# Gathers of a pairwise recommender tower issued in short runs: the first couples in twos, the rest paced by VectorE's product count

## What is computed

```python
e = jnp.stack([tbl_0[ids[:, 0]], tbl_1[ids[:, 1]], ..., tbl_39[ids[:, 39]]], axis=1)   # 512 x 40 x 64
p = e[:, rowidx]                      # the 780 pairs i < j
q = e[:, colidx]
z = jnp.einsum('bie,fie,bif->bi', p, param, q)     # param: 64 x 780 x 64
h = jnp.concatenate([z, dense_ctx], axis=1)
h = jnp.maximum(h @ W_top1 + b_top1, 0.0)
h = jnp.maximum(h @ W_top2 + b_top2, 0.0)
y = h @ W_top3
```

## Time and profile before

| | us |
|---|---|
| median of 3 runs | 548.67 (548.06 to 549.01) |
| the profiled execution | 548.24 |
| its span | 546.4 |
| TensorE matmul busy | 322.2 (59%) |
| VectorE busy | 258.1 (47%) |
| ScalarE busy | 255.2 (47%) |
| GpSimd busy | 185.2 (34%) |

### The profile page before, as it was taken

One profiled execution on the slowest core, in us unless ns is written; L12 is line 12 of the kernel. 1 busy time (PEld: TensorE's weight loads), 2 busy tenths in 40 slices (PEclk: granted clock), 3 DMA queues, 4 the chain that ended last, 5 costly groups with the idle time before them and its releaser, 6 DMA issues.

```text
span 546.4 us, 7416 instructions
## 1 busy us (share of the span) xinstructions
PE 322.2 (59%) x2318; PEld 165.8 (30%) x2318; DVE 258.1 (47%) x262; ACT 255.2 (47%) x1961; POOL 185.2 (34%) x192
## 2 busy tenths in 40 slices
PE   0402000220003200299999999899779999999988
PEld 0201000000001000155455544454454344444645
DVE  0000000000000000389899988855437999998590
ACT  1000000000002100389999969734687999995632
POOL 6777777777777760000000000000001122232030
PEclk9998555565555755599999999999889999999999
DMA  2221111211112110174324220032124242420000
GB/s 59 46 50 30 26 26 26 55 26 26 26 25 62 26 26 1 39 268 124 125 89 148 88 95 10 11 92 76 46 95 173 95 143 79 172 95 1 1 2 0
DMA packets 12937, 35.60 MB, mean 65 GB/s; under 512 B 4705, under 2 KB 5985, under 8 KB 11618
## 3 DMA queue, kind: packets, MB, share of 16 engines
q1 hardware_dynamic: 7778, 29.88, 16.4%
q0 software_dynamic: 5120, 5.25, 5.0%
HBM read 35.12 MB, written 0.00 MB: 64 GB/s over the span
## 4 chain that ended last, share of the span: by engine, by line
PE 34%; another core or an unknown queue 24%; issue 19%; ACT 13%; DVE 8%; POOL 1%; DMA 1%; DVEq 0%
ACT prod L658 11%; PE upsum L537 9%; PE upsum L532 7%; DVE prod L622 6%; PE zbank L489 6%; PE abank L444 5%; PE abank L423 1%; DVE z L596 1%; POOL emb L396 1%; PE upsum L501 1%; ACT xT L637 1%; PE upsum L505 1%; PE abank L469 1%; PE upsum L573 1%
## 5 line engine op out<-in xcount | busy, mean ns | idle before, releaser
L658 ACT ACTIVATE prod<-prod 128x64 f32<-128x64 f32 x944 | 227.0, 250 | 8.1 <-issue 7.2
L658 ACT ACTIVATION_READ_ACCUMULATOR prod<-prod 128x1 f32 x944 | 185.3, 196 | 7.7 <-issue 7.7
L396 POOL DMA_INDIRECT emb<-tbl,rows_id x160 | 151.5, 947 | 50.2 <-issue 48.5
L622 DVE TENSOR_TENSOR prod<-upsum,emb 128x1024 f32<-128x1024 f32 x98 | 116.8, 1220 | 107.1 <-remote 68.5
L537 PE MATMUL upsum<-w,xT 64*128 64x512 f32 x392 | 106.0, 641 | 102.3 <-issue 59.1
L405 POOL TENSOR_TENSOR prod<-prod 128x512 f32<-128x512 f32 x26 | 32.9, 1271 | 290.4 <-DVE prod L622 290.4
L622 DVE TENSOR_TENSOR prod<-upsum,xT 128x1024 f32<-128x1024 f32 x82 | 97.7, 1219 | 67.2 <-remote 40.0
L637 ACT ACTIVATE xT<-abank 128x256 f32<-128x256 f32 x40 | 15.1, 378 | 220.1 <-remote 129.3
L532 PE MATMUL upsum<-xT,w 64*128 64x256 f32 x656 | 88.3, 397 | 4.9 <-DVE prod L622 2.6
L537 PEld LDWEIGHTS upsum<-w,xT 64*128 64x128 f32 x392 | 33.8, 191 | 140.3 <-issue 81.2
L532 PEld LDWEIGHTS upsum<-xT,w 64*128 64x128 f32 x656 | 60.3, 190 | 35.9 <-issue 16.8
(11 more groups left out here) (46 smaller groups left out, 132.0 us busy)
## 6 DMA issues: line engine op xcount, KB each, us to landing
w<-W_top SPq DMA_DIRECT2D x2, 1792.0 KB, 8.2
emb<-tbl,rows_id POOLq DMA_INDIRECT x160
w<-param SPq DMA_DIRECT2D x2, 1248.0 KB
w<-param SPq DMA_DIRECT2D x2, 1152.0 KB
w<-param SPq DMA_DIRECT2D x2, 1120.0 KB
w<-param SPq DMA_DIRECT2D x2, 1024.0 KB
w<-param SPq DMA_DIRECT2D x2, 992.0 KB
w<-param SPq DMA_DIRECT2D x2, 896.0 KB
```

The lines of the kernel that those rows point to most:

```text
L396: pool.indirect_dma_start(emb[:, c, f, :], None, tables[f], bass.IndirectOffsetOnAxis(ap=rows_id[:, c, f:f + 1].bitcast(U32), axis=0),).th ...
L622: dve.tensor_tensor(to.rearrange("p (h q) -> p h q", h=2), t[:], f.broadcast_to([P, 2, BANK]), ALU.mult).then_inc(multiplied, 1)
L658: last = act.activation(ring[:, x * E:(x + 1) * E], ring[:, x * E:(x + 1) * E], ACT.Copy, accum_out=z_view(u)[:, x:x + 1])
```

## The change

The gathers are no longer one row. The first ten couples of half 0 are issued as before, but ahead of couples 2, 4, 6 and 8 GpSimd waits until the four gathers of the couple before have landed (so at most eight are under way). The other 30 couples move into GpSimd's loop over the units, each with a wait until VectorE has finished `u` units (`multiplied`): couples 10 to 19 of half 0, and of half 1, 20 units before their stretch; couples 0 to 9 of half 1 at units 22, 28, 34 and so on to 76, among those of half 0. `H_LAG` goes from 3 to 4. The number of gathers, their size and the order within a couple stay.

```diff
-H_LAG = 3
+H_LAG = 4
+GATHER_FIRST, GATHER_AHEAD, GATHER_OTHER, GATHER_STEP = 10, 20, 22, 6
...
+    gather_at = {}
+    for q in range(NQ):
+        s, n = stretches[q]["s"], stretches[q]["n"]
+        if s == 0 and n >= GATHER_FIRST or s == 1:
+            at = stretches[q]["first"] - GATHER_AHEAD
+            if s == 1 and n < GATHER_FIRST:
+                at = GATHER_OTHER + GATHER_STEP * n
+            assert at <= stretches[q]["first"] - GATHER_AHEAD
+            gather_at.setdefault(max(at, 0), []).append((s, n))
...
-            for s in range(HALVES):
-                for n in range(NC):
-                    for f in (2 * n, 2 * n + 1):
-                        for c in range(s * PER, (s + 1) * PER):
-                            pool.indirect_dma_start(
-                                emb[:, c, f, :], None, tables[f],
-                                bass.IndirectOffsetOnAxis(ap=rows_id[:, c, f:f + 1].bitcast(U32), axis=0),
-                            ).then_inc(gathered[s][n], 16)
+
+            def gather(s, n):
+                for f in (2 * n, 2 * n + 1):
+                    for c in range(s * PER, (s + 1) * PER):
+                        pool.indirect_dma_start(
+                            emb[:, c, f, :], None, tables[f],
+                            bass.IndirectOffsetOnAxis(ap=rows_id[:, c, f:f + 1].bitcast(U32), axis=0),
+                        ).then_inc(gathered[s][n], 16)
+
+            for n in range(GATHER_FIRST):
+                if n >= 2 and n % 2 == 0:
+
+                    pool.wait_ge(gathered[0][n - 1], 16 * 2 * PER)
+                gather(0, n)
             for u in range(NU):
+                for s, n in gather_at.get(u, []):
+
+                    if u:
+                        pool.wait_ge(multiplied, u)
+                    gather(s, n)
                 if units[u]["by"] == "H":
```

## The result

| | before | changed |
|---|---|---|
| median, us | 548.47 (548.06 to 549.01) | 452.51 (449.02 to 453.68) |
| ratio, with its interval | | 0.8239 (0.8194 to 0.8285) |
| profiled execution | 548.24 | 452.29 |
| its span | 546.4 | 450.5 |
| mean granted clock of TensorE | 0.838 | 0.913 |

The change is faster by 17.6%. The forecast was 402 us with a range of 370 to 450: the direction was right, the size was not, and the median lies 2.5 us above the range.

A forecast was written before the change was run, and what follows sets the result against it. It took late TensorE hand-offs, while gathers issued every 1.25 us are worked off at 1.40, to bound the kernel. Span 546.4 - 181 (unit 18 earlier) + 35 (paced-row freezes) = 400.4, plus 1.8 outside: 402 us, range 370 to 450.

The forecast's parts named there:

- the two harmless amounts: Backlog said to delay nothing: up to 1.6 us before unit 18; 10 or 11 gathers per round up to unit 84.
- the freeze: Until 227.68 us in the kernel before, TensorE's reports of ended instructions reach other engines at one per 1.40 us.
- never passes the 1.6 us that did no harm: First ten couples: eight gathers take 11.4 us, are worked off in 11.2, so backlog stays harmless; unit 18 at 63 us.
- rival 4: Whole loop: each group of four gathers freezes it, landing included, 6.5 us for each of 30 groups; 562 us, chance 0.06.
- Units 0 to 17 need some 17 x 1.5 = 26 us of these 60: Before unit 18: the earlier units' work fits within the first ten couples' gather time, so the product stands at 63 us.
- the same harmless eleven: Units 18 to 84: of each 14 to 16 gathers, 10 or 11 harmless, then 7 us frozen; five rounds, 35 us.
- Rival 2: Paced row freezes nearly all through, some 90 of 112 us: 457 us, from 440 to 485; chance 0.10.
- Four fall behind by 0.6 us and have the rest to recover: nothing: Late couples, units 105 to 170: four gathers about every 11 us recover their backlog, cost nothing; 56 us without that cover.
- adds no work: Halvings and H_LAG: the longer lag only moves a reduction by one place on VectorE, costed at 0.
- Rival 1: Whole kernel: short rows never fall far enough behind, so no freeze at all; 371 us, chance 0.14.
- Rival 5: Start of the program: the freeze is unconnected to the gathers and ends at 228 us regardless; 548 us, chance 0.03.
- Rival 3: Paced row: gathers slow to 2.5 us each beside a busy VectorE, 18 couples take 180 us; 461 us, chance 0.06.

The follow-up runs named there:

- e14: The changed kernel as it is, in a set without the freeze: 378.97 us, ratio 1.0297 to the kernel before (367.75).
- e5: The kernel before with H_LAG 4 instead of 3, in a set without the freeze: 370.81 us, ratio 1.0069.
- e12: The kernel before with a 512-column GpSimd memset behind each gather (1.66 us apart, one row), in a set with the freeze: 402.8 us, ratio 0.7349.
- e13: All gathers spaced by 512-column memsets, 35 couples in one row, last five 20 units ahead, H_LAG 4; set without the freeze: 387.25 us, ratio 1.0535.
- e15: The changed kernel with couples 0 to 9 of half 1 at units 40 to 94 instead of 22 to 76, without the freeze: 374.7 us, ratio 1.0231.
- e6: The changed kernel with H_LAG 3 instead of 4, in a set without the freeze: 376.74 us, ratio 1.0263 to the kernel before.
- e7: The kernel before with gathers of 64 rows instead of 128 and a memset of emb ahead, in a set without the freeze: 370.54 us, ratio 1.0088.
- e2: The kernel before with a 384-column GpSimd memset behind each gather (1.55 us apart, one row), in a set with the freeze: 410.72 us, ratio 0.7482.
- e17: All gathers spaced by 512-column memsets, 35 couples in one row, five among the halvings, H_LAG 4; set with the freeze: 387.81 us, ratio 0.7085.
- e4: The changed kernel without its four landing waits, the other 30 couples still paced, in a set with the freeze: 454.69 us, ratio 0.8283.
- e3: The kernel before with landing waits after every eight gathers through all 160, no pacing, in a set with the freeze: 511.17 us, ratio 0.9312.
- e10: The kernel before with gathers of 64 rows instead of 128 and a memset of emb ahead, in a set with the freeze: 555.39 us, ratio 1.0133.

## Why the forecast was right in direction and wrong in size

The steps that failed are the two harmless amounts in the sum, at unit 18 and up to unit 84, and a zero at its end. By the table of stretches, the changed kernel took 50 us more than the forecast: 25 by unit 18, 14 up to unit 84, 0 up to 104, 7 up to 170, 5 to the end. The changed kernel against e14, its own trace without the freeze, has 17.0, 49.2, 0, 6.1 and 0.6 us more, together 73 of the 450.5. The forecast had 35 of these, all between units 18 and 84.

**Unit 18: 88 us instead of 63.** The gathers were issued as forecast: couple 9's last ends at 59.4 (49.67 + 7 x 1.25 + 0.95; forecast 58.8). Two steps behind it failed. First, the step by which the backlog "never passes the 1.6 us that did no harm". The first two pieces do run free, but the product at 42.59 already stands at 39.81 in e14, and the one at 50.50, released by `remote`, at 41.86: 2.8 us are lost around the third piece (26.63 to 36.34), and 6 more by the fourth (38.12 to 47.83). Then come the 16 gathers in a row that I had counted as eight. The harmless start was read from a stretch in which TensorE had next to nothing to report, and carried over to one in which it had. The text named this doubt itself, in rival 4; that TensorE's activity makes the difference is likely, but no run isolates it. Second, "Units 0 to 17 need some 17 x 1.5 = 26 us of these 60" took them for done by the time that couple 9 is there. They were not. TensorE stood from 57 to 73, for a copy that ScalarE made 3.4 us after the last of the 16 gathers:

```profile
72.80 0.38 ACT L662 ACTIVATE xT<-abank 128x256 f32<-128x256 f32 x1 [15.59 <-remote]
73.24 0.69 PE L526 MATMUL upsum<-xT,w 64*64 64x256 f32 x1 [16.08 <-ACT xT L662]
```

Units 11 to 17 were still ahead, and they took the 15.3 us from 72.76 to 88.07.

e14 has its unit 18 at 71.1, so the difference of the two traces is 17 us and not 25. But the 8 us between 63 and 71 have a reason of their own there. A 1.8 MB load of the first layer's weights (L387), with 0.5 MB for the second layer just ahead of it, starts at 52.20, just as couple 8's gathers are under way:

```profile
52.20 0.51 SPq L387 DMA_DIRECT2D w<-W_top  x1
```

```profile
55.00:57.50 2.50, 0.00 (x0) 0.00 (x0) 0.00 (x0) 0.04 (x1) 1.89 (x3) 0.62 1.10 424
57.50:60.00 2.50, 0.00 (x0) 0.00 (x0) 0.00 (x0) 0.00 (x0) 1.89 (x3) 0.50 0.94 392
```

```profile
60.93 0.69 PE L448 MATMUL abank<-ident,emb 128*128 128x128 f32 x2 [7.50 <-DMA emb<-tbl,rows_id]
```

The DMA engines are full at 392 to 424 GB/s, TensorE, VectorE and ScalarE stand, and couple 8, whose last issue ended at 54.14 and would have landed at 55.6, is turned at 60.93: 5 us late. Units 14 to 17 follow it before unit 18 can. The kernel before has the same gap without a freeze (7.07 us in e5), and in e5, e12, e13, e14 and e15 couple 8 is turned 8.7 to 9.2 us after this load starts, though its gathers end anywhere from 47.9 to 62.2. In the changed kernel with the freeze the same load starts only at 74.96, 20 us after couple 8's gathers, and holds back nothing that unit 18 needs:

```profile
74.96 0.50 SPq L387 DMA_DIRECT2D w<-W_top  x1
```

So the load is no part of the 25 us measured; it is what a kernel meets there once the freeze is gone.

**Units 18 to 84: 139 us instead of 125.** The mechanism was the one forecast: gathers almost without a pause, a loop frozen in pieces. But I gave each round of 16 gathers 7 us by the same harmless eleven; 49 us were lost. Rival 2 had this stretch at 90 us of freeze and the kernel at 457. The measured 452.5 came close to its time by another way: 49 of its 90 us of freeze here, the rest elsewhere.

**Units 104 to the end: 12 us more.** "Four fall behind by 0.6 us and have the rest to recover: nothing" was nearly right: 6 us up to unit 170, and 2 more right behind it (units 170 to 180 take 14.8 us instead of 12.9). The rest is `H_LAG`, by which the forecast's step "adds no work" failed: e5 is slower by 0.69% (370.81 to 366.91). All of it lies behind the start of the last unit. There the span has 14.65 us left with lag 3 (before, e6, e7), and with lag 4 between 15.8 and 18.7:

```profile
356.70:372.48 15.78, 12.53 (x70) 8.15 (x70) 1.22 (x2) 3.58 (x9) 0.00 (x0) 1.00 0.00 0
```

```profile
359.07:377.72 18.65, 15.41 (x70) 9.24 (x70) 1.21 (x2) 3.58 (x9) 0.00 (x0) 0.82 0.00 0
```

The first is e15, the second e14, with the same instructions on TensorE and VectorE. The lag itself costs 1.1 us, and 1.6 to 2.9 more where the granted clock is at its lower level for a part of the stretch (mean 0.82 in e14, 0.90 in the changed kernel and e5, 1.00 in e15). Before it TensorE has waited 1.91 us for the last reduction, in e15 as in e14, against 0.18 in e6; what decides between the two clocks is not shown. Lag 3 gives back 1.8 us at the halvings that stand behind gathers (e6 against e14).

**Rivals 1, 3 and 5.** Rival 1 (no freeze, 371) describes the sets without the freeze, where the changed kernel takes 379: 8 us more than rival 1 said, which is the 8 us at unit 18; `H_LAG` and the 4 us that I had allowed for late couples cancel. Rival 5 had the freeze end at 228 us whatever the gathers do; e2 and e12 refute it, since the gathers' distance alone takes the freeze away. Rival 3 fell: gathers beside a busy VectorE keep 0.94 to 0.95 us each (e14, e17).

**What the waits for landings were good for:** beside the pacing, nothing measured (e4). Alone they took 37 us off the kernel before, but no more, since a piece of eight is long enough to freeze the loop (e3). Without the freeze, they and `H_LAG` are the change's cost: unit 18 at 71.1 in e14 against 65.5 in e5 for the waits, and the last stretch for the lag.

**What stays open.** What works gathers off at one per 1.40 us, why reports of other engines wait meanwhile, and what separates the two conditions is not shown. At intervals above 1.40 us the backlog can't grow from gathers alone, yet 1.55 still lost 26 us between units 18 and 84 and 1.66 none. That the reports share the same time with the gathers would fit; no run here tests it. One thing in the trace of the kernel before speaks against engines taking turns at one server, and I had overlooked it: late in the freeze the engines' own instructions go at this pace, and two engines at once.

```profile
183.48 0.27 PE L423 MATMUL abank<-ident,emb 128*128 128x128 f32 x1 [2.21 <-issue]
186.28 0.37 PE L423 MATMUL abank<-ident,emb 128*128 128x128 f32 x1 [2.53 <-issue]
```

```profile
190.46 0.20 ACT L658 ACTIVATION_READ_ACCUMULATOR prod<-prod 128x1 f32 x1 [1.14 <-issue]
191.86 0.26 ACT L658 ACTIVATE prod<-prod 128x64 f32<-128x64 f32 x1 [1.20 <-issue]
193.27 0.20 ACT L658 ACTIVATION_READ_ACCUMULATOR prod<-prod 128x1 f32 x1 [1.15 <-issue]
```

TensorE's two transposes, each with its weight load, are 2.80 us apart, so 1.40 per instruction. Of ScalarE's instructions, 0.2 to 0.3 us long, eleven follow that of 178.56 up to 193.27, across both transposes: eight of them at 1.39 to 1.41 us, the others at 0.7, 0.7 and 2.1. So more is late than the reports, and each engine seems to have a pace of its own of about one instruction per 1.40 us. Why stays open.

A kernel that spaces only the gathers issued beside busy engines, and so would cost less without the freeze, wasn't tried.

## To carry to other kernels

Before moving work around a slow stretch, measure what makes it slow by one edit that changes only that: a half-microsecond memset behind each gather took the whole freeze away and told more than the reordering. A "harmless" amount read from idle engines is no bound for busy ones. And time a kernel in several sets before tuning to one: this change is 18% faster under one condition of the chip and 3% slower under the other.

## What the runs showed of the hardware

- One program takes 548 us in some sets of runs and 367 in others, steady within each. The trace's mark of the freeze is `remote` as the releaser of products and copies; the lists of waits of e5 and e14 (without it) and of e12 and e17 (gathers 1.65 us apart, in the sets with it) hold none.
- With the freeze, indirect gathers are worked off at 1.40 us per DMA, for 128 rows (224.5 us for 160, before) as for 64 (223.8, e10); in e10 the last 16 are also issued 1.40 apart, by the reckoning above with about 19 outstanding.
- The loop's hand-offs freeze with gathers 1.25 and 1.34 us apart, nearly recover at 1.55 (410.72 us) and fully at 1.65 (387.81 us in a set with the freeze, 387.25 in one without).
- Late in the freeze TensorE's and ScalarE's own instructions are started about one per 1.40 us (183.48 to 186.28 and 190.46 to 193.27, before).
- Beside a 1.8 MB load, with the DMA engines at 392 to 424 GB/s, a couple's four gathers were waited for 5 us beyond the usual landing (e14); in four more traces (e5, e12, e13, e15) couple 8 is likewise turned 8.7 to 9.2 us after the load's start.
- The end of the program, the same 70 matmuls, took 15.78 us at a granted clock of 1.00 (e15) and 18.65 at 0.82 (e14).
- A memset of 128 x 512 on GpSimd takes 0.54 us, of 128 x 128 0.22 us; a gather of 128 rows occupies it for 0.95 us and the next follows 0.30 us later, with or without a busy VectorE.
